# Latent cross-attention block of a two-layer decoder: the transposes of two key groups issued together every other step, and the row sums of a unit in one instruction

## The chip, the cores and the metric

One Trainium2 chip, one core of it. The metric is device microseconds for one execution of the whole program, a decoder of two layers. Three executions of the kernel before took 1926.25, 1928.07 and 1931.09 us; their median is 1928.07.

## What is computed

The program runs six blocks one after the other, each followed by a layer norm: windowed attention, cross-attention and a mixture of experts in layer 0, then grouped attention, latent cross-attention and a second attention with experts in layer 1. The change lies in the latent cross-attention alone. Cut to that block, the reference is:

```
x: (4, 256, 256)   kv_c: (4, 1601, 64)   H = 16 heads
q_big  = rope((x @ Wq.T) @ w_kc_q)                # 192 wide per head
kv_r   = rope(kv_c)
scores = (q_big @ W_qr) . (kv_r @ W_kr)           # per head: 256 x 1601
attn   = softmax(scores, axis=-1)
ctx    = (attn @ kv_r) @ w_kc_kv.T                # per head
x      = layernorm(x + concat_heads(ctx) @ Wo.T)
```

## The kernel before, in words

The block works in **units**: a unit is one head and one batch entry, so there are N = 16 x 4 = 64 of them. A unit has 256 query rows, held as two halves of 128 rows (index `i` = 0 or 1), and 1601 keys. The kernel folds W_qr and W_kr into one matrix per head, so that scores are formed straight against the roped latent keys, which are kept for all batch entries in on-chip memory (`e_KT` for the scores, `e_kv` for the context). Products are made in two or three passes of a high and a low part (`_hi`, `_lo`): ScalarE rounds a result to the high part, VectorE subtracts to get the low part.

Per unit the work is:

- **score(u, i, j)** (line 2521, TensorE): scores of half i against piece j of the keys; the pieces are 304, 496, 496 and 305 keys wide. Two products each. It writes PSUM bank j and must wait until the exponential that read this bank last is done (`exped.at(s - 3)`).
- **maximum(u, i, j)** (line 2692, VectorE): row maximum of a piece; after piece 3 a small reduction over the four maxima (line 2699) releases the exponentials.
- **exponential(u, i, j)** (line 2627, ScalarE): exp of a piece with its row sum, written to `e_P`.
- **turn(u, g)** (line 2537, TensorE): the probabilities are transposed, keys to partitions, in seven groups g of 256 keys (GROUPS = 7; the last has 65 keys). Groups 0 to 5 take four 128x128 transposes each, group 6 two. A group goes to one of two PSUM banks (`tb_bank`), in turns, and so waits until the low part of the group two before it has been formed.
- **upper_pt(u, g)** (line 2641, ScalarE) copies the turned group to `e_PT_hi`, **lower_pt(u, g)** (line 2709, VectorE) forms `e_PT_lo`.
- **attend(u, g)** (line 2551, TensorE): the context gets the products of group g, four of them (two for group 6).
- **absorb_q, project_q, fold_q / fold_r / fold_o, project_out** (TensorE): the query of the next unit against the folded matrix, the query of the unit after that, the folding of the next head's weights (one of the three in three units of every four), and the context through the output matrix. **add** (line 2722, VectorE) adds the projected context, scaled by the reciprocal of the row sum, to X. **row_sums** (line 2701, VectorE) adds the four partial sums of a half and takes the reciprocal.

The order is written out by hand. Each engine runs a loop over i = 0 .. N + 2 (lines 2584, 2654 and 2741), with u = i, v = i - 1, w = i - 2 and after = i + 1, and eight steps in each turn of the loop. In a **step** TensorE does, in this order: turn(v, step) for steps 0 to 6; attend of the group three steps behind (LAG = 3, so groups 5 and 6 of unit w in steps 0 and 1, groups 0 to 4 of unit v in steps 3 to 7); score(u, 1, j) in steps 0 to 3 or score(after, 0, j) in steps 4 to 7; then absorb_q in step 1, project_q in step 3, a fold in step 5, project_out in step 7. ScalarE does exponential, then the context or query copies, then upper_pt(v, step). VectorE does the context, query and sum work, then maximum, then lower_pt(v, step). All engines take their instructions in order and wait on semaphores; there is no queue of DMAs in this loop but the fetch of a head's weights by SyncE, once in four units.

The waits that the change touches are these:

```python
def turn(u, g):
    at, p = GROUPS * u + g, Pm[u % 2]
    ...
    pe.wait_ge(*exped.at(8 * u + 8))
    if at >= 2:
        pe.wait_ge(*pt_lo.at(at - 1))     # group at - 2 has its low part
```

Of the kernel before, what the change touches and what calls it, by code (L numbers as in the profile page):

```python
# [12 lines left out]
ALU = mybir.AluOpType  # L13
ACT = mybir.ActivationFunctionType
AX = mybir.AxisListType
# [39 lines left out]
def decoder(nc, t, out):  # L55
    with ExitStack() as top:
        pe, act, dve, pool, sp = nc.tensor, nc.scalar, nc.vector, nc.gpsimd, nc.sync

        def sem(name):
            return top.enter_context(nc.semaphore(name))  # L60
# [34 lines left out]
        link = Count(sem("dve_link"))  # L95
# [213 lines left out]
        def enter_tensor(b, k):  # L309
            pe.wait_ge(xt_source, b + 1)  # L310
            turn_tensor(normed[b], k)
# [2115 lines left out]
        def latent_attention(latent, before, following):  # L2427
# [8 lines left out]
            GROUPS = -(-KT // 2)  # L2436
# [6 lines left out]
            with ExitStack() as sc:  # L2443
# [3 lines left out]
                def S_(n):  # L2447
                    return signal(n)
# [11 lines left out]
                scored, maxed, exped = S_("scored"), S_("maxed"), S_("exped")  # L2460
# [3 lines left out]
                def a_unit(i):  # L2464
                    return i if 0 <= i < N else None
# [5 lines left out]
                def keys_of(g):  # L2471

                    return min(2, KT - 2 * g), min(P, CTX - 2 * g * P)
# [12 lines left out]
                def tensor():  # L2486
                    free = [None]

                    def aux_bank():
                        if free[0]:  # L2490
                            pe.wait_ge(*free[0])
                        return bank[aux]
# [44 lines left out]
                    def turn(u, g):  # L2537
                        at, p = GROUPS * u + g, Pm[u % 2]
                        o = bank[tb_bank[at % 2]]
                        n, rows = keys_of(g)  # L2540
                        pe.wait_ge(*exped.at(8 * u + 8))
                        if at >= 2:
                            pe.wait_ge(*pt_lo.at(at - 1))
                        for c in range(n):
                            k0 = (2 * g + c) * P
                            for i in range(2):
                                last = pe.transpose(o[0:rows, c * SEQ + i * P:c * SEQ + (i + 1) * P],  # L2547
                                                    p[:, i, k0:k0 + rows], ident[:])
                        last.then_inc(*turned.up())

                    def attend(u, g):
                        at = GROUPS * u + g
                        x = PT[at % PT_BUFS]
                        n, rows = keys_of(g)
                        if g == 0:
                            if u == 0:
                                pe.wait_ge(*latent.kv_lo.at(BATCH))
                            else:
                                pe.wait_ge(*cx_lo.at(u))
                        pe.wait_ge(*pt_lo.at(at + 1))  # L2560
                        for c in range(n):
                            for y in range(2):
                                last = mm(bank[ctx_bank][:, 0:SEQ], kvb[u % BATCH][0:rows, 2 * g + c, :], x[y][0:rows, c, :],
                                          g == 0 and c == 0 and y == 0, g == GROUPS - 1 and c == n - 1 and y == 1)
                        last.then_inc(*attended.up())
# [18 lines left out]
                    for i in range(N + 3):  # L2584
                        u, v, w, after = a_unit(i), a_unit(i - 1), a_unit(i - 2), a_unit(i + 1)
                        h, quarter = i // BATCH + 1, i % BATCH
                        for step in range(8):
                            half, j = divmod(step, 4)
                            if v is not None and step < GROUPS:
                                turn(v, step)  # L2590
                            if step == 2 and i == N:
                                enter_tensor(0, enter_bank)
                            if step < LAG and w is not None and step - LAG + 8 < GROUPS:
                                attend(w, step - LAG + 8)
                            if step >= LAG and v is not None:
                                attend(v, step - LAG)
                            if half == 0 and u is not None:
                                score(u, 1, j)
                            elif half == 1 and after is not None:
                                score(after, 0, j)  # L2600
                            if step == 1 and after is not None:
                                absorb_q(after)
                            if step == 3 and i + 2 < N:
                                if i + 2 == BATCH - 1:
                                    aux_bank()
                                    norm_tensor(12 + BATCH - 1, BATCH - 1, aux)
                                    free[0] = (xt_lo, 12 + BATCH)
                                project_q(i + 2)
                            if step == 5 and h < H and quarter < 3:
                                (fold_q, fold_r, fold_o)[quarter](h)  # L2610
                            if step == 7 and w is not None:
                                project_out(w)
# [73 lines left out]
                def vector():  # L2686
# [11 lines left out]
                            dve.wait_ge(link.sem, link.step())  # L2698
                            dve.tensor_reduce(s[:, i, 4:5], s[:, i, 0:4], AX.X, ALU.max, negate=True).then_inc(*maxed.up())  # L2699

                    def row_sums(u, i):
                        s = st[u % 4]
                        dve.wait_ge(*exped.at(8 * u + 4 * i + 4))
                        dve.tensor_reduce(s[:, i, 5:6], s[:, i, 0:4], AX.X, ALU.add).then_inc(link.sem, 1)
                        dve.wait_ge(link.sem, link.step())
                        dve.reciprocal(s[:, i, 6:7], s[:, i, 5:6]).then_inc(link.sem, 1)
                        link.step()

                    def lower_pt(u, g):
# [31 lines left out]
                    for i in range(N + 3):  # L2741
                        u, v, w, after = a_unit(i), a_unit(i - 1), a_unit(i - 2), a_unit(i + 1)
                        h, quarter = i // BATCH + 1, i % BATCH
                        for step in range(8):
                            half, j = divmod(step, 4)
                            if step == LAG - 1 and w is not None:
                                lower_context(w)
                            if step == 4 and v is not None:
                                row_sums(v, 1)
                            if step == 4 and u is not None:  # L2750
                                row_sums(u, 0)
                            if step == 2 and after is not None:
                                lower_qk(after)
                            if step == 0 and 3 <= i <= N + 1:
                                add(i - 3)
                            if step == 6 and h < H and quarter < 3:
                                (latent.lower_q, latent.lower_r, latent.lower_o)[quarter](h, bank[aux])
                            if half == 0 and u is not None:
                                maximum(u, 1, j)
                            elif half == 1 and after is not None:  # L2760
                                maximum(after, 0, j)
                            if v is not None and step < GROUPS:
                                lower_pt(v, step)
                            if step == 3 and i + 2 == BATCH - 1:
                                for part_ in range(4):
                                    norm_vector(BATCH - 1, tiny[BATCH - 1], part_)
                                norm_lower(12 + BATCH, BATCH - 1, aux)
                            if i == N - 1 and step >= 3:
                                if step == 3:
                                    dve.wait_ge(*x_added.at(N - BATCH + 1))  # L2770
                                enter_vector(0, step - 3, rows=True)
                            if i == N and step == 3:
                                scaled_lower(16 + 1, 0, enter_bank, 0)
                            if i == N and step == 7:
                                dve.wait_ge(*x_added.at(N - BATCH + 2))
                                enter_vector(1, 0, bank[enter_place])
                            if i == N + 1 and step in (2, 3, 4):
                                enter_vector(1, step - 1, bank[enter_place])
# [184 lines left out]
```

## Time and profile before

| | |
|---|---|
| median of three runs | 1928.07 us (1926.25 to 1931.09) |
| profiled execution, first to last instruction (span) | 1919.4 us |
| TensorE busy with products / with weight loads | 1791.9 us (93%) / 1490.5 us (78%) |
| VectorE / ScalarE / GpSimd busy | 1282.1 us (67%) / 1088.8 us (57%) / 686.3 us (36%) |
| mean granted TensorE clock | 0.979 of full speed |
| transposes of the probabilities, `bank<-ident,e_P` at line 2547 | 1664, first at 796.0 us, last at 1612.6 us |

The page of the profiled execution gives its span and no other time of its own; the median of the runs is 8.7 us above that span. The latent block fills the time from about 785 to 1615 us. PE is TensorE at products, PEld TensorE loading weights (a product's stationary operand, which overlaps the product before), DVE VectorE, ACT ScalarE. A matmul's record begins when the engine takes it up and ends when its result has landed, so records of neighbours overlap: what an instruction costs in a dense stretch is the distance from its start to the next one's. A transpose appears as a MATMUL with `ident`.

### The profile page before, as it was taken

The numbers are of one execution on the slowest core, as the hardware profiler recorded it, in microseconds if no ns is written. First come the engines' busy times: TensorE is split into PE (matmuls) and PEld (weight loads), VectorE is DVE, ScalarE is ACT, GpSimd is POOL, SyncE is SP. The second block draws the span as 40 slices with busy tenths as digits, with TensorE's granted clock in tenths as the row PEclk, the third lists the DMA queues.
The fourth block names the chain that finished last, engine by engine and source line by source line (L and its number), as shares of the span: only waits on it lengthen the run. The fifth ranks groups of instructions, "written<-read, shape, count | busy, mean of one in ns | idle before, by whom it ended". The sixth has DMA issues, their size and how long they took to land.

```text
span 1919.4 us, 42082 instructions
## 1 busy us (share of the span) xinstructions
PE 1791.9 (93%) x15752; PEld 1490.5 (78%) x15752; DVE 1282.1 (67%) x3335; ACT 1088.8 (57%) x2750; POOL 686.3 (36%) x674
## 2 busy tenths in 40 slices
PE   7999998889998998699999999999999998898995
PEld 6999977646656776599999999999999997674663
DVE  5676657742237666488888888888888888775222
ACT  4766654312213333488888888888888885531221
POOL 5643322132223532344433444344433441123221
PEclk8999999989999999899999999999999999999998
DMA  4000019222328000000000000000000001402223
GB/s 165 23 2 1 1 55 359 69 93 45 45 54 266 11 3 2 22 12 12 12 12 12 28 12 12 12 12 12 12 2 12 1 2 72 204 2 81 46 47 66
DMA packets 51861, 91.69 MB, mean 48 GB/s; under 512 B 4592, under 2 KB 43632, under 8 KB 49232
## 3 DMA queue, kind: packets, MB, share of 16 engines
q1 hardware_dynamic: 42928, 78.16, 12.1%
q0 software_dynamic: 8160, 10.29, 3.5%
q8 instruction: 130, 2.13, 0.5%
q10 hardware_dynamic: 576, 0.56, 0.1%
q14 instruction: 67, 0.55, 0.1%
HBM read 56.13 MB, written 32.87 MB: 46 GB/s over the span
## 4 chain that ended last, share of the span: by engine, by line
PE 77%; DVE 11%; ACT 6%; issue 2%; DMA 2%; POOL 2%; SPq 0%; DVEq 0%; ACTq 0%; POOLq 0%
PE bank L100 63%; PE bank L2547 10%; ACT d_PT L1339 2%; ACT landing L1339 2%; PE bank L1160 1%; PE bank L1888 1%; DVE a_t L707 1%; PE bank L505 1%; PE bank L1867 1%; DVE tiny L133 1%; DVE X L172 1%; DVE d_nm L1427 1%; DVE tiny L128 0%; DVE a_t L704 0%; DMA c_sums<-c_y,c_xs 0%
## 5 line engine op out<-in xcount | busy, mean ns | idle before, releaser
L2695 DVE TENSOR_REDUCE e_st<-bank 128x1 f32<-128x496 f32 (+2 forms) x512 | 291.6, 570 | 122.1 <-PE bank L100 121.0
L2632 ACT ACTIVATE e_P<-bank,e_st 128x496 f32<-128x496 f32 (+2 forms) x512 | 307.2, 600 | 94.5 <-DVE e_st L2699 92.9
L2714 DVE TENSOR_TENSOR e_PT_lo<-bank,e_PT_hi 128x512 fp32r<-128x512 f32 (+1 forms) x448 | 287.2, 641 | 1.5 <-ACT e_PT_hi L2647 1.4
L2547 PE MATMUL bank<-ident,e_P 128*128 128x128 f32 (+1 forms) x1664 | 258.3, 274 | 4.2 <-DVE e_PT_lo L2714 3.7
L2647 ACT CAST e_PT_hi<-bank 128x512 fp32r<-128x512 f32 (+1 forms) x448 | 248.5, 555 | 10.7 <-PE bank L2547 6.6
L100 PE MATMUL bank<-e_PT_hi,e_kv 128*128 128x256 f32 (+1 forms) x832 | 249.0, 320 | 0.0
L2547 PEld LDWEIGHTS bank<-ident,e_P 128*128 128x128 f32 (+1 forms) x1664 | 194.9, 140 | 31.0 <-issue 26.3
L100 PE MATMUL bank<-e_PT_lo,e_kv 128*128 128x256 f32 (+1 forms) x832 | 215.6, 279 | 0.0
L100 PE MATMUL bank<-e_KT,e_qk_hi 128*128 128x496 f32 (+2 forms) x512 | 199.0, 389 | 7.2 <-ACT e_P L2632 5.7
L100 PE MATMUL bank<-e_KT,e_qk_lo 128*128 128x496 f32 (+2 forms) x512 | 177.1, 346 | 0.0
L100 PEld LDWEIGHTS bank<-e_PT_lo,e_kv 128*128 128x128 f32 (+1 forms) x832 | 158.4, 190 | 2.4
L100 PEld LDWEIGHTS bank<-e_PT_hi,e_kv 128*128 128x128 f32 (+1 forms) x832 | 157.6, 189 | 2.2
L100 PE MATMUL bank<-mask_b,ident_b 128*128 128x128 bf16 (+2 forms) x924 | 132.5, 271 | 11.3 <-DVE d_nm L1429 6.8
L100 PEld LDWEIGHTS bank<-e_KT,e_qk_hi 128*128 128x128 f32 x512 | 95.9, 187 | 30.0 <-ACT e_P L2632 20.3
L2394 POOL TENSOR_TENSOR e_r<-x_in,e_ropeq 96x512 f32<-96x512 f32 x32 | 40.9, 1279 | 217.6 <-ACT x_in L2315 217.6
L2394 POOL TENSOR_TENSOR x_in<-x_in,e_ropeq 96x512 f32<-96x512 f32 x32 | 41.0, 1281 | 205.0 <-ACT x_in L2315 205.0
L100 PEld LDWEIGHTS bank<-mask_b,ident_b 128*128 128x128 bf16 x924 | 71.0, 99 | 49.8 <-DVE d_nm L1429 8.5
L2632 ACT ACTIVATION_READ_ACCUMULATOR e_P<-bank,e_st 128x1 f32 x512 | 102.6, 200 | 0.0
L1532 POOL TENSOR_SCALAR_AFFINE_SELECT landing<-landing 128x768 f32<-128x768 f32 x64 | 39.5, 642 | 168.4 <-ACT landing L1339 168.4
L100 PEld LDWEIGHTS bank<-e_KT,e_qk_lo 128*128 128x128 f32 x512 | 96.9, 189 | 0.1
L1339 ACT ACTIVATE d_PT<-bank 128x1536 f32<-128x1536 f32 x32 | 46.5, 1452 | 86.6 <-PE bank L100 86.6
L1339 ACT ACTIVATE landing<-bank 128x1536 f32<-128x1536 f32 x32 | 46.4, 1451 | 81.4 <-PE bank L100 81.4
(470 smaller groups left out, 4955.9 us busy)
## 6 DMA issues: line engine op xcount, KB each, us to landing
c_wall<-in_c_w SPq DMA_DIRECT2D x8, 1536.0 KB, 18.9
g_wall<-in_g_w SPq DMA_DIRECT2D x8, 1536.0 KB, 19.1
c_rows<-normed SPq DMA_DIRECT2D x9, 1040.0 KB, 12.8
g_rows<-normed SPq DMA_DIRECT2D x9, 1040.0 KB, 13.5
e_stage<-in_e_w SPq DMA_DIRECT2D x16, 416.0 KB, 3.2
c_xs<-c_rows SPq DMA_DIRECT2D x23, 130.0 KB, 2.1
g_xs<-g_rows SPq DMA_DIRECT2D x23, 130.0 KB, 2.1
landing<-in_a_wo SPq DMA_DIRECT2D x2, 1024.0 KB, 6.0
```

What stands on the lines that cost most here:

```text
L100: return pe.matmul(o, a, b, start=start, stop=stop, skip_group_check=True)
L133: stats = dve.bn_stats(T[:, 6 * i:6 * i + 6], X[:, 2 * b + i, :])
L172: normed = dve.tensor_scalar(X[:, 2 * b + i, :], X[:, 2 * b + i, :], T[:, 12 + 2 * i:13 + 2 * i], T[:, 18 + i:19 + i], ALU.subtract, ALU.mult)
L505: last = pe.transpose(o[:, r * P:(r + 1) * P], p[:, r * P:(r + 1) * P], ident[:])
L1339: act.activation(PT[n % 2].rearrange("p a j n -> p (a j n)"), psum[:, B_BANK:B_BANK + 3, :].rearrange("p a n -> p (a n)"), ACT.Exp, scale= ...
L1532: last = pool.affine_select(blocks, blocks, pattern=pattern, compare_op=ALU.is_ge, fill=0.0, base=0, channel_multiplier=-1)
L2394: pool.tensor_tensor(x1, v, self.ropeq[:, 0:2, :], ALU.mult)
L2547: last = pe.transpose(o[0:rows, c * SEQ + i * P:c * SEQ + (i + 1) * P], p[:, i, k0:k0 + rows], ident[:])
L2632: act.activation(Pm[u % 2][:, i, STARTS[j]:STARTS[j] + n], bank[score_bank[j]][:, 0:n], ACT.Exp, bias=s[:, i, 4:5], accum_out=s[:, i, j:j ...
L2647: act.copy(PT[at % PT_BUFS][0][0:rows, 0:n, :], bank[tb_bank[at % 2]][0:rows, 0:n * SEQ].rearrange("p (c n) -> p c n", c=n)).then_inc(*pt_ ...
L2695: last = dve.tensor_reduce(s[:, i, j:j + 1], bank[score_bank[j]][:, 0:PIECES[j]], AX.X, ALU.max)
L2714: dve.tensor_tensor(lo, bank[tb_bank[at % 2]][0:rows, 0:n * SEQ].rearrange("p (c n) -> p c n", c=n), hi.bitcast(F32), ALU.subtract).then_i ...
```

## The change

TensorE's turns are issued two groups at a time: at steps 0, 2 and 4 the groups (0, 1), (2, 3) and (4, 5), at step 6 group 6 alone. Everything else of a step stays where it was, so group 1 is turned one step earlier than before (ahead of attend(w, 5) and score(u, 1, 0)), group 3 ahead of score(u, 1, 2), and group 5 ahead of attend(v, 1) and score(after, 0, 0). The copies on ScalarE and VectorE stay one to a step. The number of transposes is the same, and so are the two banks and the waits of each turn.

VectorE's row_sums takes both halves of a unit in one pair of instructions: at step 4 the sums of unit v, both halves, instead of half 1 of unit v and half 0 of unit u.

```diff
@@ tensor()
                         for step in range(8):
                             half, j = divmod(step, 4)
-                            if v is not None and step < GROUPS:
-                                turn(v, step)
+                            if v is not None and step % 2 == 0:
+                                for g in range(step, min(step + 2, GROUPS)):
+                                    turn(v, g)
@@ vector()
-                    def row_sums(u, i):
+                    def row_sums(u):
                         s = st[u % 4]
-                        dve.wait_ge(*exped.at(8 * u + 4 * i + 4))
-                        dve.tensor_reduce(s[:, i, 5:6], s[:, i, 0:4], AX.X, ALU.add).then_inc(link.sem, 1)
+                        dve.wait_ge(*exped.at(8 * u + 8))
+                        dve.tensor_reduce(s[:, :, 5], s[:, :, 0:4], AX.X, ALU.add).then_inc(link.sem, 1)
                         dve.wait_ge(link.sem, link.step())
-                        dve.reciprocal(s[:, i, 6:7], s[:, i, 5:6]).then_inc(link.sem, 1)
+                        dve.reciprocal(s[:, :, 6], s[:, :, 5]).then_inc(link.sem, 1)
                         link.step()
...
                             if step == 4 and v is not None:
-                                row_sums(v, 1)
-                            if step == 4 and u is not None:
-                                row_sums(u, 0)
+                                row_sums(v)
```

## Rows read from the trace of the kernel before

**Rows 1.** The page: its span, and the chain that ended last, by line

```profile
span 1919.4 us, 42082 instructions
...
PE bank L100 63%; PE bank L2547 10%; ACT d_PT L1339 2%; ACT landing L1339 2%; PE bank L1160 1%; PE bank L1888 1%; DVE a_t L707 1%; PE bank L505 1%; PE bank L1867 1%; DVE tiny L133 1%; DVE X L172 1%; DVE d_nm L1427 1%; DVE tiny L128 0%; DVE a_t L704 0%; DMA c_sums<-c_y,c_xs 0%
```

**Rows 2.** Busy time by stretch: PE, PEld, DVE, ACT, POOL, granted clock, DMA share, GB/s

```profile
1200.00:1300.00 100.00, 100.00 (x745) 92.19 (x744) 84.31 (x204) 82.16 (x222) 40.79 (x40) 1.00 0.04 11
```

**Rows 3.** Timeline, TensorE products, one turn of the loop: start, us, what

```profile
1199.91 0.60 PE L2547 MATMUL bank<-ident,e_P 128*128 128x128 f32 x4
...
1200.47 0.28 PE L100 MATMUL bank<-e_PT_lo,e_kv 128*128 128x256 f32 x1
1200.59 0.28 PE L100 MATMUL bank<-e_PT_hi,e_kv 128*128 128x256 f32 x1
...
1200.97 0.41 PE L100 MATMUL bank<-e_KT,e_qk_hi 128*128 128x304 f32 x1
...
1201.35 0.60 PE L2547 MATMUL bank<-ident,e_P 128*128 128x128 f32 x4
...
1202.11 0.49 PE L100 MATMUL bank<-e_KT,e_qk_hi 128*128 128x496 f32 x1
...
1203.37 0.60 PE L2547 MATMUL bank<-ident,e_P 128*128 128x128 f32 x4
...
1204.28 0.63 PE L2547 MATMUL bank<-ident,e_P 128*128 128x128 f32 x4
...
1206.96 0.60 PE L2547 MATMUL bank<-ident,e_P 128*128 128x128 f32 x4
...
1209.06 0.39 PE L100 MATMUL bank<-e_KT,e_qk_hi 128*128 128x496 f32 x1
...
1209.52 0.81 PE L100 MATMUL bank<-e_stage 128*128 128x192 f32 x4
...
1212.78 0.60 PE L2547 MATMUL bank<-ident,e_P 128*128 128x128 f32 x4
```

**Rows 4.** Timeline, TensorE's weight loads: score(u, 1, 0), and the turn of group 3

```profile
1200.97 0.19 PEld L100 LDWEIGHTS bank<-e_KT,e_qk_hi 128*128 128x128 f32 x1 [0.19 <-ACT e_P L2632]
...
1204.25 0.42 PEld L2547 LDWEIGHTS bank<-ident,e_P 128*128 128x128 f32 x4 [0.24 <-issue]
```

**Rows 5.** Timeline, ScalarE: exponentials of both halves

```profile
1201.28 0.69 ACT L2632 ACTIVATE e_P<-bank,e_st 128x496 f32<-128x496 f32 x1
1201.85 0.21 ACT L2632 ACTIVATION_READ_ACCUMULATOR e_P<-bank,e_st 128x1 f32 x1
...
1206.58 0.52 ACT L2632 ACTIVATE e_P<-bank,e_st 128x304 f32<-128x304 f32 x1 [1.00 <-DVE e_st L2699]
```

**Rows 6.** Timeline, VectorE: maxima, low parts and row sums of the same stretch

```profile
1202.86 0.68 DVE L2695 TENSOR_REDUCE e_st<-bank 128x1 f32<-128x496 f32 x1 [0.24 <-PE bank L100]
1203.45 0.68 DVE L2714 TENSOR_TENSOR e_PT_lo<-bank,e_PT_hi 128x512 fp32r<-128x512 f32 x1
...
1204.71 0.66 DVE L2695 TENSOR_REDUCE e_st<-bank 128x1 f32<-128x496 f32 x1
...
1206.46 0.68 DVE L2714 TENSOR_TENSOR e_PT_lo<-bank,e_PT_hi 128x512 fp32r<-128x512 f32 x1
...
1207.32 0.14 DVE L2704 TENSOR_REDUCE e_st<-e_st 128x1 f32<-128x4 f32 x1
...
1208.35 0.47 DVE L2695 TENSOR_REDUCE e_st<-bank 128x1 f32<-128x304 f32 x1 [0.69 <-PE bank L100]
...
1211.52 0.68 DVE L2695 TENSOR_REDUCE e_st<-bank 128x1 f32<-128x496 f32 x1
```

**Rows 7.** Timeline, TensorE products, experts of layer 0: six transposes on end

```profile
427.13 0.60 PE L1888 MATMUL bank<-ident,c_h 128*128 128x128 f32 x4
427.56 0.38 PE L1867 MATMUL bank<-ident,c_xs 128*128 128x128 f32 x2
```

**Rows 8.** Timeline, TensorE products, last unit, with no scores between the turns

```profile
1607.63 0.63 PE L2547 MATMUL bank<-ident,e_P 128*128 128x128 f32 x4 [0.35 <-DVE e_PT_lo L2714]
```

## The prediction

> **What bounds the kernel now.** I read the page first: in the chain that ended last TensorE's products at L100 and its transposes of probabilities at L2547 hold 73% of the span [rows 1]. Then the busy time by stretch: in the latent block TensorE is at products all the time, at full granted clock (1.00, the 2.4 GHz level), with VectorE at 84% and ScalarE at 82% [rows 2]. So this block is bound by TensorE's queue, and the question is where that queue waits. The timeline of one turn of the loop shows it. The turn runs from one turn(v, 0), at 1199.91, to the next, at 1212.78: 12.87 us [rows 3]. I measure costs there by distance between starts.
>
> First, what a transpose costs. Four in a record of 0.60, each some 0.27 long, gives (0.60 - 0.27) / 3 = 0.11 apart. The second product behind the block at 1199.91 starts at 1200.47, 0.56 later, and the next one 0.12 after it [rows 3]. Four transposes at 0.11 and one product at 0.12 are 0.56. So nothing is left over for changing from transposing to multiplying.
>
> Second, where it waits. score(u, 1, 0) should start at 1200.59 + 2 x 0.12 = 1200.83. Its weights are loaded at 1200.97, after 0.19 idle for an exponential [rows 4], and the next turn starts at 1201.35 where 1201.11 was due (a pair of 304 columns streams in 0.28): **about 0.25 lost**. Then score(u, 1, 1) starts at 1202.11. Behind four transposes (0.44) and attend(w, 6) (two products, 0.23) it was due at 1201.35 + 0.67 = 1202.02. Its release is the end of exponential(u, 0, 1) with its read-out, 1201.85 + 0.21 = 1202.06 [rows 5]. This wait loses about 0.2: 0.09 of lateness, and some 0.10 for a weight load that no product hides (the record of its first product is 0.49 long, that of the same shape at 1209.06 only 0.39 [rows 3]). Last, the turn of group 3: its weights are loaded at 1204.25, PEld idle 0.24 before [rows 4]. lower_pt(v, 1), which it must wait for, runs on VectorE from 1203.45 to 1204.13 [rows 6]. So it starts 0.12 after its releaser: **the turn of group 3 has no slack today**. The profile calls that idle time "issue"; the code's wait on pt_lo and the last unit, where such a turn is shown waiting 0.35 for e_PT_lo [rows 8], tell me which it is.
>
> **Part by part, in the middle of the block.** Times are those of the rows.
>
> *Fewer, longer blocks of turns.* Seven blocks become four. By the sum above a switch costs 0.00; the rounding of the rows leaves at most 0.01 for each, 0.03 x 2 for a unit. I take nothing. Here the Trainium skill speaks for the change: "TensorE: Matmul & The Clock Gate", section "Back-to-back issue gap", gives about 81 ns for each load and matmul of 128 columns in a sustained stream, which would make 0.65 of eight turns. Six transposes on end in another block are still 0.11 apart (427.13 to 427.56 is four of them) [rows 7]; the trace does not agree, and I keep 0.11. It is a rival below.
>
> *Group 1 one step earlier.* Its 0.44 now stands ahead of attend(w, 5) and score(u, 1, 0), whose wait of 0.25 it fills. But the turn stood between score(u, 1, 0) and score(u, 1, 1) before, so what TensorE does ahead of score(u, 1, 1) is the same work. That score is held by exponential(u, 0, 1), which doesn't look at the turns (ScalarE takes it before it copies group 1). TensorE would be there at about 1201.77 and waits to 1202.11 as before. **Gain: 0.** The wait moves and grows to 0.33.
>
> *Group 3 ahead of score(u, 1, 2).* The path to its release is score(u, 1, 1), then maximum (VectorE from 1202.86), then lower_pt(v, 1) to 1204.13, then 0.12 [rows 6, 4]. None of it moves. TensorE is through with group 2 at 1203.37 + 0.44 = 1203.81 and then stands for 0.44 until 1204.25, where before it did score(u, 1, 2). The turn starts at 1204.28, as before, and score(u, 1, 2) comes after it. A pair of that width costs 1209.52 - 1209.06 = 0.46 [rows 3]. So all that follows is later by **0.46**.
>
> *Group 5 ahead of attend(v, 1).* It waits for lower_pt(v, 3). VectorE's chain now starts from the late score(u, 1, 2): 1204.28 + 0.44 + 0.46 = 1205.18 for its stream; from the end of a stream to its maximum takes 0.19 (score(u, 1, 1): 1202.11 + 0.10 for the bare load + 0.46 = 1202.67, maximum at 1202.86), so 1205.37 where it was 1204.71. From that maximum's start to the end of lower_pt(v, 3) VectorE works back to back, 1206.46 + 0.68 - 1204.71 = 2.43, so it ends at 1207.80, and the turn's weights come at 1207.92. TensorE has group 4 at 1206.96 + 0.46 = 1207.42 and is through at 1207.86. Another **0.06 to 0.12** of waiting. I take 0.10.
>
> *What hangs on both.* The exponentials of half 1 start later by 0.66 (the maximum's delay): 1206.58 becomes 1207.24, and they share ScalarE with the copy of the projected query. score(after, 0, 1) needs the second of them at about the time that TensorE reaches it. Bounds are 0 and 0.10; I take 0.04. The sum at the end of the turn is 0.46 + 0.10 + 0.04 = 0.60.
>
> *Is it given back?* TensorE has 0.33 of waiting at score(u, 1, 1), so a late TensorE alone would recover part. But the exponentials that it waits for start from maximum(after, 0, 2) and (after, 0, 3). VectorE takes maximum(after, 0, 2) at 1211.52 [rows 6], within 0.04 of the landing of its score, and is busy without a gap from there. So those exponentials are late by the same 0.60, and the turn of the loop is longer by all of it.
>
> *Row sums.* Two small instructions of about 0.15 and their links fall away on VectorE [rows 6]. Behind them VectorE is idle 0.69, until score(after, 0, 0) is there [rows 6]. Cost and gain 0; with the change that idle time only grows. The wait for exponential(u, 0, 3) goes too, in front of the same idle time. The sums are needed two turns later.
>
> *DMAs* do not move. Unit 63's turns have no scores beside them and already wait for low parts [rows 8]; I count nothing there.
>
> **Sum.** 64 units give 63 turns of the loop with both scores and turns: 63 x 0.60 = 38 us. Against the profiled execution: 1919.4 + 38 = 1957. The median of the runs lies 8.7 us above that span, so 1928.07 + 38 = **1966 us**. Bounds of the unknown terms: 0.42 a turn (the delay of 0.46 less some 0.04 of smaller waits that it covers, no more waiting at group 5) gives 26 us; 0.75 (0.46, 0.19 at group 5, 0.10 at the score) gives 47 us: 1954 to 1975.
>
> **Rivals.**
> (a) *The covered wait wins: faster.* Place: score(u, 1, 0) and (u, 1, 1), price 0.25 + 0.2 a turn, 63 x 0.45 = 28 us, 1900 us. It decides if lower_pt(v, 1) ends 0.44 before today's 1204.13, so that group 3 finds its bank free. For it: the waits are real. Against: VectorE can't take lower_pt(v, 1) before maximum(u, 1, 1), which has waited for its score [rows 6]. Chance 0.06.
> (b) *It does nothing that can be seen.* TensorE's stall at group 3 would have to be given back wholly at later waits. Those there, 0.2 at score(u, 1, 1) and hundredths elsewhere, hold less than half of 0.60. It would also come out so if the engine ran the scores past a turn that waits. 1928 us, chance 0.06.
> (c) *Longer blocks run faster.* Turns after the first go down to the time 128 columns stream, 0.46 / 2 x 128 / 496 = 0.06. That saves 0.05 on each of eight turns in groups 3 to 5 that aren't followed by a wait: 0.60 - 0.40 = 0.20, 13 us, 1941 us. The skill's 81 ns would give half of that saving, some 1953 us. Chance 0.04.
> (d) *The late scores are partly recovered*, since the exponentials have slack that I don't see: 0.60 - 0.33 = 0.27, 17 us, 1945 us. Chance 0.08.
> My forecast has 0.76. A measurement of this kernel can tell 0.3%, about 6 us. (a) is faster, (b) the same; (c), (d) and the forecast are slower: 0.06, 0.06, 0.88. The range is the forecast's own, drawn down towards (c) and (d): 1948 to 1976.
>
> **What would show it.** Right: PEld's turn of groups 2 and 3 shows about 0.4 idle between them, from e_PT_lo; score(u, 1, 2) starts behind group 3; the wait before score(u, 1, 0) is gone and that before (u, 1, 1) is 0.3 or more; one turn of the loop takes about 13.5 where it took 12.87; VectorE's and ScalarE's busy shares fall by some 4%. Wrong: transposes in a block of eight closer than 0.11, groups 2 and 3 without a gap, or lower_pt(v, 1) ending before maximum(u, 1, 1) has begun.

## Result and profile after

The changed kernel takes 1975.05 us (median of four, 1973.31 to 1975.66) where the kernel before took 1927.96 in the same comparison: **1.0249 times as long, 95% interval 1.0233 to 1.0266**, 47 us slower. The forecast was slower, 1966 us, 38 us over; the range 1948 to 1976 held the time.

The profiled execution of the changed kernel spans 1972.1 us. From its page, the span, the chain that ended last by line, and two groups of instructions (busy, mean ns of one | idle before, releaser); L2696 is the maximum and L2547 the turn:

```profile
span 1972.1 us, 41954 instructions
...
PE bank L100 46%; DVE e_st L2696 8%; PE bank L2547 6%; DVE e_PT_lo L2715 6%; ACT e_P L2633 4%; ACT d_PT L1339 2%; ACT landing L1339 1%; PE bank L1160 1%; PE bank L1888 1%; DVE a_t L707 1%; PE bank L505 1%; ACT e_PT_hi L2648 1%; DVE e_st L2700 1%; PE bank L1867 1%; DVE d_nm L1427 0%
...
L2696 DVE TENSOR_REDUCE e_st<-bank 128x1 f32<-128x496 f32 (+2 forms) x512 | 292.1, 571 | 187.2 <-PE bank L100 183.4
...
L2547 PE MATMUL bank<-ident,e_P 128*128 128x128 f32 (+1 forms) x1664 | 250.4, 276 | 34.1 <-DVE e_PT_lo L2715 28.9
```

Before, the chain held TensorE's two lines at 73% and no line of the latent block on another engine among those shown [rows 1]. Now 20% of the span runs through the latent block's lines on VectorE and ScalarE (8% maxima, 6% low parts, 4% exponentials, 1% each for the small reductions and for the copies), and TensorE's two lines have 52%. The turns wait, by the profile's own naming, 28.9 us for `e_PT_lo`. Busy time by stretch says the same; TensorE was at 100.00 here [rows 2]. The clock is unchanged:

```profile
1200.00:1300.00 100.00, 95.29 (x702) 86.62 (x701) 78.46 (x177) 76.45 (x208) 37.54 (x36) 1.00 0.04 12
```

Two turns of the loop of the changed kernel on TensorE, products only. The first, from 1213.15, has no fold in it; the second, from 1226.54, has fold_q (`e_stage`), as the turn of rows 3 had:

```profile
1213.15 1.04 PE L2547 MATMUL bank<-ident,e_P 128*128 128x128 f32 x8
...
1223.18 0.39 PE L100 MATMUL bank<-e_KT,e_qk_lo 128*128 128x496 f32 x1
1223.89 0.41 PE L2547 MATMUL bank<-ident,e_P 128*65 128x128 f32 x2 [0.33 <-ACT e_P L2633]
...
1226.54 1.03 PE L2547 MATMUL bank<-ident,e_P 128*128 128x128 f32 x8
1230.00 0.60 PE L2547 MATMUL bank<-ident,e_P 128*128 128x128 f32 x4
1230.90 0.63 PE L2547 MATMUL bank<-ident,e_P 128*128 128x128 f32 x4 [0.30 <-DVE e_PT_lo L2715]
1233.99 1.25 PE L2547 MATMUL bank<-ident,e_P 128*128 128x128 f32 x8
1236.76 0.81 PE L100 MATMUL bank<-e_stage 128*128 128x192 f32 x4
1237.42 0.38 PE L2547 MATMUL bank<-ident,e_P 128*65 128x128 f32 x2
1240.03 1.04 PE L2547 MATMUL bank<-ident,e_P 128*128 128x128 f32 x8
```

Read the second against [rows 3], from one turn(v, 0) to the next. Group 2 comes 3.46 after it, as before (1203.37 - 1199.91): the earlier group 1 gained nothing. Group 3 comes 0.90 behind group 2 though the four transposes of group 2 take 0.44, so TensorE stands for 0.46. Group 4 comes at 7.45 where it came at 7.05: 0.40 late. The block of groups 4 and 5 lasts 1.25 and not 1.04, so group 5 waits 0.21. The turn of the loop ends at 13.49 where it ended at 12.87: **0.62 more**.

The turn without a fold took 12.27 in the kernel before and takes 1226.54 - 1213.15 = 13.39 now: **1.12 more**. Here are the two starts in the kernel before:

```profile
1238.36 0.60 PE L2547 MATMUL bank<-ident,e_P 128*128 128x128 f32 x4
...
1250.63 0.60 PE L2547 MATMUL bank<-ident,e_P 128*128 128x128 f32 x4
```

The difference between the two kinds of turn is the wait before group 6, at 1223.89. The last product ahead of it starts at 1223.18 and streams 0.23, so group 6 was due at 1223.41 and is 0.48 late. (In the turn of the kernel before it was 0.04 late.) How much longer a turn is depends on its kind in all of the block, not only in these two. From the starts of turn(v, 0) in both timelines, the turns i = 3 to 61, medians by kind in us (a fold is missing in every fourth turn and in all turns of the last head):

| fold in step 5 | turns | before | changed | more |
|---|---|---|---|---|
| fold_q | 14 | 12.89 | 13.49 | 0.60 |
| fold_r | 14 | 12.97 | 13.57 | 0.60 |
| fold_o | 14 | 12.64 | 13.37 | 0.73 |
| none | 17 | 12.31 | 13.37 | 1.06 |

TensorE's weight loads show the three waits beside one another, at groups 3, 5 and 6, with the wait for score(u, 1, 1) ahead of them:

```profile
1215.36 0.19 PEld L100 LDWEIGHTS bank<-e_KT,e_qk_hi 128*128 128x128 f32 x1 [0.40 <-ACT e_P L2633]
1217.51 0.42 PEld L2547 LDWEIGHTS bank<-ident,e_P 128*128 128x128 f32 x4 [0.50 <-issue]
1221.22 0.42 PEld L2547 LDWEIGHTS bank<-ident,e_P 128*128 128x128 f32 x4 [0.23 <-ACT e_P L2633]
1223.86 0.19 PEld L2547 LDWEIGHTS bank<-ident,e_P 128*65 128x65 f32 x2 [0.72 <-issue]
```

VectorE in the same turn:

```profile
1216.12 0.68 DVE L2696 TENSOR_REDUCE e_st<-bank 128x1 f32<-128x496 f32 x1
1216.71 0.68 DVE L2715 TENSOR_TENSOR e_PT_lo<-bank,e_PT_hi 128x512 fp32r<-128x512 f32 x1
...
1220.43 0.68 DVE L2715 TENSOR_TENSOR e_PT_lo<-bank,e_PT_hi 128x512 fp32r<-128x512 f32 x1
1221.02 0.15 DVE L2705 TENSOR_REDUCE e_st<-e_st 128x2 f32<-128x8 f32 x1
1221.21 0.17 DVE L2707 RECIPROCAL e_st<-e_st 128x2 f32<-128x2 f32 x1
1222.68 0.47 DVE L2696 TENSOR_REDUCE e_st<-bank 128x1 f32<-128x304 f32 x1 [1.30 <-PE bank L100]
1223.07 0.68 DVE L2715 TENSOR_TENSOR e_PT_lo<-bank,e_PT_hi 128x512 fp32r<-128x512 f32 x1
```

Each wait has its low part: 1216.71 + 0.68 = 1217.39, and group 3's weights come 0.12 later; 1220.43 + 0.68 = 1221.11, and group 5's come 0.11 later; 1223.07 + 0.68 = 1223.75, and group 6's come 0.11 later. For the last two the profile's "issue" and "ACT e_P" are not the releaser. All three low parts stand behind a maximum, and the third maximum is that of score(after, 0, 0), for which VectorE is idle 1.30 (0.69 before [rows 6]). Some 0.25 of that growth is only the shorter row sums; the rest is the score, which is now behind the turn of group 5: from the start of the low part of group 3 to this maximum there were 1208.35 - 1206.46 = 1.89 and are 1222.68 - 1220.43 = 2.25.

### The profile page after: what moved, and what is told of

It is laid out like the page before. It is cut to its first block, busy times and chain, and to the rows that moved or that the text cites. A ratio compares the mean times of both kernels' runs of the same rounds, so it can differ in the third digit from the quotient of the medians.

```text
span 1972.1 us, 41954 instructions
## 1 busy us (share of the span) xinstructions
PE 1804.5 (92%) x15752; PEld 1489.5 (76%) x15752; DVE 1270.5 (64%) x3207; ACT 1081.2 (55%) x2750; POOL 686.3 (35%) x674
## 4 chain that ended last, share of the span: by engine, by line
PE 56%; DVE 23%; ACT 10%; issue 7%; DMA 2%; POOL 2%; SPq 0%; ACTq 0%; DVEq 0%; POOLq 0%
PE bank L100 46%; DVE e_st L2696 8%; PE bank L2547 6%; DVE e_PT_lo L2715 6%; ACT e_P L2633 4%; ACT d_PT L1339 2%; ACT landing L1339 1%; PE bank L1160 1%; PE bank L1888 1%; DVE a_t L707 1%; PE bank L505 1%; ACT e_PT_hi L2648 1%; DVE e_st L2700 1%; PE bank L1867 1%; DVE d_nm L1427 0%
## 5 line engine op out<-in xcount | busy, mean ns | idle before, releaser
L2696 DVE TENSOR_REDUCE e_st<-bank 128x1 f32<-128x496 f32 (+2 forms) x512 | 292.1, 571 | 187.2 <-PE bank L100 183.4
L2547 PE MATMUL bank<-ident,e_P 128*128 128x128 f32 (+1 forms) x1664 | 250.4, 276 | 34.1 <-DVE e_PT_lo L2715 28.9
L2547 PEld LDWEIGHTS bank<-ident,e_P 128*128 128x128 f32 (+1 forms) x1664 | 185.4, 141 | 76.0 <-issue 55.5
L100 PE MATMUL bank<-e_PT_hi,e_kv 128*128 128x256 f32 (+1 forms) x832 | 232.3, 300 | 0.0
L100 PE MATMUL bank<-e_KT,e_qk_hi 128*128 128x496 f32 (+2 forms) x512 | 190.5, 372 | 17.0 <-ACT e_P L2633 15.8
```

The source lines that it names most:

```text
L100: return pe.matmul(o, a, b, start=start, stop=stop, skip_group_check=True)
L2696: last = dve.tensor_reduce(s[:, i, j:j + 1], bank[score_bank[j]][:, 0:PIECES[j]], AX.X, ALU.max)
```

## The experiments

For each kernel I show one row, the adds to X (line L2732 or L2733): two for a unit, from the first to the last start. That time holds 63 turns of the loop and leaves the other blocks out, so it is free of what moves there. The whole times are medians against the kernel before on the same chip in the same comparison. The row of the kernel before, 788.2 us from first to last, and that of the changed kernel, 836.1, which is **47.9 more**:

```profile
L2732 DVE SCALAR_TENSOR_TENSOR X<-bank,e_st,X x128: 467/478/486, 832.3 to 1620.5; 128x256 f32<-128x256 f32 x128
```
```profile
L2733 DVE SCALAR_TENSOR_TENSOR X<-bank,e_st,X x128: 469/477/485, 836.8 to 1672.9; 128x256 f32<-128x256 f32 x128
```

All of the 47 us are in this stretch. The spans of the two profiled executions differ by 52.7; the other 4.8 lie outside it, 4.5 of them before the first add, in blocks that the change doesn't touch. Each stretch is one execution; three kernels that should not differ here (before, pair01, sums_only) have 788.2, 788.1 and 788.2.

### One pair at a time

The kernel before, with TensorE's groups by step written as a table, and one pair in it:

```diff
-                            if v is not None and step < GROUPS:
-                                turn(v, step)
+                            if v is not None:
+                                for g in {0: [0, 1], 2: [2], 3: [3], 4: [4], 5: [5], 6: [6]}.get(step, []):
+                                    turn(v, g)
```

**pair01.** 

> The kernel before with groups 0 and 1 turned together at step 0, everything else as before. Theory A (a turn costs when it comes up before the low part of the group two before it, and that low part is held behind a maximum): group 1 needs the low part of group 6 of the unit before, which is there since long; the wait before score(u, 1, 0) of 0.25 us goes and the one before score(u, 1, 1) grows by as much, because the exponential it waits for does not move. 0 us, 1928 (within 5). Rival B (a longer block of transposes costs by itself, each of the three pairs about a third of the 47 us): 1928 + 16 = 1944. Rival C (the covered wait is worth having): 63 x 0.25 = 16 us faster, 1912.

Measured: 1921.31 us against 1921.75, ratio 0.9997 (0.9981 to 1.0013). The stretch takes 788.1, 0.1 less than before.

```profile
L2733 DVE SCALAR_TENSOR_TENSOR X<-bank,e_st,X x128: 470/477/486, 831.7 to 1619.8; 128x256 f32<-128x256 f32 x128
```

A block of eight transposes costs nothing by itself, and filling the wait of 0.25 gains nothing: the interval runs from 3.7 us faster to 2.5 us slower, where rivals B and C have 16 us each.

**pair23**, with `2: [2, 3]` and single groups elsewhere. 

> The kernel before with groups 2 and 3 turned together at step 2. Theory A: this pair holds most of the loss. score(u, 1, 2) comes behind the turn of group 3, which starts no earlier than before: 0.46 us a turn of the loop, and what follows it waits on VectorE a little more (0.0 to 0.15): 63 x 0.46 to 0.61 = 29 to 38 us, 1957 to 1966. In the trace an idle time of about 0.4 on the weight loads before the turn of group 3. Rival B: 1944.

Measured: 1966.5 us against 1921.75, ratio 1.0224 (1.02 to 1.0249). The stretch takes 824.7, **36.5 more**, 0.58 a turn. The whole time says 43, with an interval from 38 to 48. The profiled execution is 50.2 longer in span, and 13.7 of that lie outside the stretch, 7.9 of them behind it, where the granted clock was 0.92 from 1690 to the end (0.95 from 1640 to the end in the kernel before). Nothing was changed there, so I go by the stretch.

```profile
L2733 DVE SCALAR_TENSOR_TENSOR X<-bank,e_st,X x128: 466/477/486, 838.1 to 1662.8; 128x256 f32<-128x256 f32 x128
```

Its turn of group 3 waits just as in the changed kernel, 0.90 behind group 2:

```profile
1200.13 0.60 PE L2547 MATMUL bank<-ident,e_P 128*128 128x128 f32 x4
1201.03 0.63 PE L2547 MATMUL bank<-ident,e_P 128*128 128x128 f32 x4 [0.30 <-DVE e_PT_lo L2715]
```

That accounts for some 0.40 of the 0.58 (group 4 comes 1204.11 - 1200.13 = 3.98 behind group 2, where it came 1206.96 - 1203.37 = 3.59). The rest is a wait at score(after, 0, 1) for exponential(u, 1, 1), which is late by the same chain:

```profile
1206.04 0.20 ACT L2633 ACTIVATION_READ_ACCUMULATOR e_P<-bank,e_st 128x1 f32 x1
...
1206.10 0.28 PE L100 MATMUL bank<-e_PT_lo,e_kv 128*128 128x256 f32 x1
1206.29 0.49 PE L100 MATMUL bank<-e_KT,e_qk_hi 128*128 128x496 f32 x1
```

The exponential's read-out ends at 1206.24. The score was due at 1206.10 + 0.12 = 1206.22, starts 0.07 later, and its first record is 0.49 long and not 0.39: 0.17 lost. In the changed kernel this score doesn't wait, because TensorE has by then waited 0.21 at group 5.

**pair45**, with `4: [4, 5]` and single groups elsewhere. 

> The kernel before with groups 4 and 5 turned together at step 4. Theory A: the low part of group 3 ends at 1207.14 in the trace of before, the turn of group 4 ends its stream at 1207.40, so group 5 does not wait here. What is late is score(after, 0, 0), by the 0.44 of the group ahead of it; its maximum and the low part of group 4 behind it are late too, and the turn of group 6 needs that low part: at most 0.1 to 0.3 a turn, and less where a fold stands before group 6: 0 to 15 us, 1928 to 1943. Rival B: 1944. If it costs nothing at all, the wait at group 6 in the changed kernel comes only from the pairs together.

Measured: 1930.75 us against 1921.75, ratio 1.0057 (1.0028 to 1.0085). The stretch takes 797.1, **8.9 more**, 0.14 a turn.

```profile
L2733 DVE SCALAR_TENSOR_TENSOR X<-bank,e_st,X x128: 468/478/486, 832.2 to 1629.3; 128x256 f32<-128x256 f32 x128
```

The block of eight is 1.03 long, group 5 does not wait, and in the turn without a fold group 6 does. Both are rows of TensorE's timeline:

```profile
1201.02 0.41 PE L2547 MATMUL bank<-ident,e_P 128*65 128x128 f32 x2 [0.33 <-DVE e_PT_lo L2715]
...
1210.70 1.03 PE L2547 MATMUL bank<-ident,e_P 128*128 128x128 f32 x8
```

So this pair delays the score that a low part is queued behind, and the turn of group 6 pays. The pairs add up to 0 + 36.5 + 8.9 = 45 of 47.9. They are not independent, though: pair23 pays 0.17 a turn at the score, where the changed kernel pays 0.21 at group 5, so the near agreement is in part chance.

### The row sums alone

**sums_only**: the changed kernel's VectorE with the single turns of the kernel before. 

> The kernel before with the row sums of both halves in one pair of instructions and single turns. Theory A: VectorE is idle 0.69 us behind the sums, so 0 us, 1928 (within 3). Rival D (the two small instructions and their waits are on VectorE's path to the next maxima): faster by up to 63 x 0.25 = 16 us, 1912.

Measured: 1920.35 us against 1921.75, ratio 0.9996 (0.9978 to 1.0014). The stretch takes 788.2, as before. VectorE does 128 instructions less and nobody notices.

```profile
L2732 DVE SCALAR_TENSOR_TENSOR X<-bank,e_st,X x128: 469/476/485, 831.4 to 1619.6; 128x256 f32<-128x256 f32 x128
```

### The low part ahead of the maximum

If the pairs cost what they do because a low part is queued behind a maximum, then VectorE's order is the place to take the wait away. In the changed kernel:

```diff
+                            first = step in (1,)
+                            if first and v is not None:
+                                lower_pt(v, step)
                             if half == 0 and u is not None:
                                 maximum(u, 1, j)
                             elif half == 1 and after is not None:
                                 maximum(after, 0, j)
-                            if v is not None and step < GROUPS:
+                            if v is not None and step < GROUPS and not first:
                                 lower_pt(v, step)
```

**pairs_low1**, as above. 

> The changed kernel, and in step 1 VectorE forms the low part of group 1 ahead of maximum(u, 1, 1) instead of behind it. Theory A: the turn of group 3 no longer stands for 0.44 us, since the low part ends near 1203.2 in the times of the kernel before and the turn comes up at 1203.81; that maximum starts 0.36 later, where VectorE had time. The waits at groups 5 and 6 (0.1 and up to 0.35 a turn) stay. 0.46 of the 0.75 lost in each turn of the loop come back, less what the later maximum costs: 20 to 29 us under the changed kernel, some 14 to 25 over the kernel before. Rival B (the long blocks cost by themselves): as slow as the changed kernel, 47 us over the kernel before.

Measured: 1939.58 us against 1921.16, ratio 1.0083 (1.0051 to 1.0115), 16 us over the kernel before and some 31 under the changed kernel. The stretch takes 805.3, 17.1 more than before and **30.8 less than the changed kernel**, a little more than the 29 expected.

```profile
L2733 DVE SCALAR_TENSOR_TENSOR X<-bank,e_st,X x128: 469/477/487, 829.2 to 1634.5; 128x256 f32<-128x256 f32 x128
```

Groups 2 and 3 are now one block without a gap, eight transposes in 1.04:

```profile
1207.85 1.04 PE L2547 MATMUL bank<-ident,e_P 128*128 128x128 f32 x8
```

The same paired turns, with the same banks: the wait was the cost, not the block.

**pairs_low4**, the changed kernel with `(4,)`. 

> The changed kernel, and in step 4 alone VectorE forms the low part of group 4 ahead of maximum(after, 0, 0). The wait of the turn of group 6, which no term of the prediction had, goes; those of groups 3 and 5 stay. If that wait is what the prediction missed, the turn of the loop falls from 13.45 to about the 13.30 foreseen: 10 us less than the changed kernel, some 37 over the kernel before. If the exponentials behind it only hand the time on to another wait: between 0 and 5 us less. Rival B (block length): no change, 47 over.

Measured: 1967.18 us against 1923.26, ratio 1.0227 (1.0213 to 1.0242). The stretch takes 825.9, **10.2 less than the changed kernel**, 37.7 over the kernel before.

```profile
L2733 DVE SCALAR_TENSOR_TENSOR X<-bank,e_st,X x128: 468/476/486, 832.4 to 1658.3; 128x256 f32<-128x256 f32 x128
```

Its turn without a fold takes 1217.41 - 1204.59 = 12.82 where the changed kernel's takes 13.39; group 3 waits as ever:

```profile
1204.59 1.03 PE L2547 MATMUL bank<-ident,e_P 128*128 128x128 f32 x8
...
1208.96 0.63 PE L2547 MATMUL bank<-ident,e_P 128*128 128x128 f32 x4 [0.30 <-DVE e_PT_lo L2715]
...
1217.41 1.03 PE L2547 MATMUL bank<-ident,e_P 128*128 128x128 f32 x8
```

**pairs_low14**, with `(1, 4)`. 

> The changed kernel with the low part ahead in steps 1 and 4: without the waits of groups 3 and 6, with that of group 5. Theory A: pairs_low1 took 12.95 us a turn of the loop against 12.70 before, and the wait of group 6 is in that; without it 12.80 to 12.87, so 6 to 11 us over the kernel before. If group 6 doesn't matter once group 3 is served: as pairs_low1, 16 us over.

Measured: 1931.62 us against 1923.26, ratio 1.0051 (1.0031 to 1.0071). The stretch takes 795.5, 7.3 over the kernel before. The wait of group 6 counts also once group 3 is served.

```profile
L2733 DVE SCALAR_TENSOR_TENSOR X<-bank,e_st,X x128: 470/478/486, 834.7 to 1630.2; 128x256 f32<-128x256 f32 x128
```

**pairs_low12456**, with `(1, 2, 4, 5, 6)`. 

> The changed kernel with the low part ahead of the maximum in steps 1, 2, 4, 5 and 6. Theory A: the low part of group 4 no longer stands behind the maximum of the late score(after, 0, 0), so the turn of group 6 doesn't wait, and none of the three waits is left. Then the paired turns cost nothing: within 6 us of the kernel before, or up to 10 us faster, since maximum(after, 0, 3) starts as soon as its score is there (0.16 us a turn). Rival B: still some 47 us over it.

Measured: 1916.0 us against 1921.16, ratio 0.9958 (0.994 to 0.9976). The stretch takes 778.2, 57.9 less than the changed kernel and **10.0 less than the kernel before**.

```profile
L2733 DVE SCALAR_TENSOR_TENSOR X<-bank,e_st,X x128: 466/476/485, 838.0 to 1616.2; 128x256 f32<-128x256 f32 x128
```

### The same order with single turns

**single_low56**: the kernel before with the low part first in steps `(5, 6)`. 

> The kernel before, single turns, with the low part ahead of the maximum in steps 5 and 6. Theory A, carried on: the scores of the next unit wait for exponentials that start from maximum(after, 0, 3), which VectorE takes at 1212.44 although its score landed at 1212.24, because the low part of group 6 stands between it and maximum(after, 0, 2). With that low part ahead, the maximum starts about 0.16 us earlier, and the waits at score(u, 1, 0) and (u, 1, 1) shrink by it: 63 x 0.16 = 10 us faster, 0.5%. Rival: those waits are set elsewhere (ScalarE), 0 us.

Measured: 1915.15 us against 1921.16, ratio **0.9951 (0.9931 to 0.9971)**, 6 to 9 us faster. The stretch takes 779.2, 9.0 less than before. The spans of the profiled executions differ by 1.4 only: the blocks outside the stretch took 7.6 longer in this one, at a mean granted clock of 0.973 against 0.979, though nothing was changed there; why is not shown.

```profile
L2732 DVE SCALAR_TENSOR_TENSOR X<-bank,e_st,X x128: 468/477/486, 836.2 to 1615.4; 128x256 f32<-128x256 f32 x128
```

**single_low6**, with `(6,)` alone. 

> The kernel before with the low part of group 6 alone ahead of maximum(after, 0, 2). If the gain of single_low56 (10 us in the turns of the loop, 6 to 12 in the whole time) comes from maximum(after, 0, 3) starting with its score, most of it is here: 6 to 10 us faster. If step 5 is needed for it (the maxima of steps 5 and 6 run back to back where a fold's low part stands between them): 2 to 4 us faster.

Measured: 1919.34 us against 1923.26, ratio 0.9975 (0.9963 to 0.9987), 4 to 5 us. The stretch takes 781.9, 6.3 less than before. So two thirds of the gain in the stretch are in step 6; step 5 gives the rest. The whole time lies between the two expectations.

```profile
L2732 DVE SCALAR_TENSOR_TENSOR X<-bank,e_st,X x128: 468/476/485, 836.1 to 1618.0; 128x256 f32<-128x256 f32 x128
```

VectorE in the kernel before has the low part of group 6 between the last two maxima. The last product of score(after, 0, 3) lands at 1211.93 + 0.30 = 1212.23, and its maximum starts 0.21 later:

```profile
1212.11 0.41 DVE L2714 TENSOR_TENSOR e_PT_lo<-bank,e_PT_hi 65x256 fp32r<-65x256 f32 x1
1212.44 0.46 DVE L2695 TENSOR_REDUCE e_st<-bank 128x1 f32<-128x305 f32 x1
```

In single_low56 that low part comes first, and the two maxima after it run on end. The last product of the same score lands at 1211.53 + 0.30 = 1211.83. The record of both maxima ends at 1212.34, so the second, 0.46 long, starts at about 1211.88, 0.05 behind its score and not 0.21:

```profile
1210.95 0.41 DVE L2714 TENSOR_TENSOR e_PT_lo<-bank,e_PT_hi 65x256 fp32r<-65x256 f32 x1
1211.28 1.06 DVE L2695 TENSOR_REDUCE e_st<-bank 128x1 f32<-128x496 f32 x2
1212.38 0.16 DVE L2699 TENSOR_REDUCE e_st<-e_st 128x1 f32<-128x4 f32 x1
```

The gain turns up where it was expected, at score(u, 1, 0): it comes 1200.54 - 1199.63 = 0.91 behind turn(v, 0), where it came 1200.97 - 1199.91 = 1.06 behind it [rows 3]. The 0.15 over 63 turns are 9.5 us.

```profile
1199.63 0.60 PE L2547 MATMUL bank<-ident,e_P 128*128 128x128 f32 x4
...
1200.54 0.40 PE L100 MATMUL bank<-e_KT,e_qk_hi 128*128 128x304 f32 x1
```

It is the fastest of the kernels here, beside pairs_low12456, which can't be told from it. I have not tried more orders.

## Why the prediction was right

**The mechanism held at each point it named.**

- *Switching between turning and multiplying costs nothing.* Eight transposes on end take 1.04, (1.04 - 0.27) / 7 = 0.11 apart, as in blocks of four; pair01 moved nothing. Rival (c), the closer spacing in long blocks, with the 81 ns that the Trainium skill gives in "TensorE: Matmul & The Clock Gate", section "Back-to-back issue gap", is out for these fp32 transposes: no block of eight here was closer than 0.11.
- *Group 1 early: 0.* pair01, 0.1 us. Rival (a) is out: the wait at score(u, 1, 0) went, and the load for score(u, 1, 1) is idle 0.40 in its place.
- *Group 3 waits for the low part behind maximum(u, 1, 1).* TensorE stood for 0.46, foreseen 0.44; what follows is late by 0.40 in the turn with fold_q, foreseen 0.46. pairs_low1 took it away and gave back 30.8 us.
- *Group 5 waits, then the score.* Foreseen 0.10 + 0.04, measured 0.21 at group 5 and nothing that shows after it. As a sum, 0.60 was foreseen for the turn with fold_q that I walked through, and 0.62 measured. The terms are not that good one by one: 0.40, 0.21 and 0 against 0.46, 0.10 and 0.04. Their errors cancel because the turn of group 5 waits for VectorE's chain, and the chain was foreseen well: the end of the low part of group 3 at 1234.46, shifted by 1226.54 - 1199.91 to the times of rows 3, is 1207.83, foreseen 1207.80.
- *Nothing is given back*: rival (d) foresaw 0.27 a turn; the two turns shown have 0.62 and 1.12, and the mean is 47.9 / 63 = 0.76.
- *Row sums: 0.* sums_only.
- *Busy shares.* In the stretch from 1200 to 1300 VectorE fell from 84.31 to 78.46 and ScalarE from 82.16 to 76.45; a fall of some 4% was foreseen, and it is larger, as is the turn of the loop.

**The term that was mis-sized is the number of turns that one turn stood for.** I took the turn of the loop from 1199.91, which has a fold in step 5, and multiplied it by 63. The walk ended at score(after, 0, 1) and went on to the end with "the sum at the end of the turn is 0.60"; it has no line for group 6, which needs the low part of group 4. In three turns of four a fold stands ahead of group 6 and covers that wait or some of it, in the fourth, and in all turns of the last head, nothing does: 1.06 instead of 0.60, and 0.73 with fold_o. Over 63 turns the step gave 38 us and the trace shows 47.9; pairs_low4, which takes the wait of group 6 away, stands at 37.7. That is the 10 us that were missing, and nearly all of the distance between 1966 and 1975. That the range still held 1975, by 1 us, is luck: none of its terms stood for this wait.

My own row had the warning: VectorE idle 0.69 until score(after, 0, 0) was there [rows 6] says that the low part behind it hangs on that score. I read it as cover for the row sums and did not ask what a late score would do to what is queued behind its maximum.

## What to carry to other kernels

When a step is moved forward in the queue of the engine that bounds the kernel, look for what releases it: if its releaser is already just in time, the engine stands still for the whole distance it was moved, and the work it passed is late by its own length. Filling an earlier wait is worth nothing while the next wait hangs on a chain that the move doesn't shorten. And walk one turn of every kind: a piece of work that comes in three turns of four may be the cover that the fourth lacks. Where such a wait has to go, the order on the releasing engine is the cheap place: the low part ahead of the maximum brought back all 48 us, and gave 0.5% even without the paired turns.

## What I had not expected of the hardware and its records

From the end of a low part on VectorE to the load of weights on TensorE that waits for it there were 0.11 to 0.12 us in every case looked at, steady enough to name the releaser by hand. The profile's own name for it was not reliable where an instruction waits for two semaphores: the wait of group 5 is put down to `e_P`, that of group 6 to "issue" on the weight loads and to `e_P` on the products, while in pair45 the same wait of group 6 is put down to `e_PT_lo`.
